# Causal mask of an attention kernel: from a TensorE product to an addition by VectorE in the bank

## The chip, the core and the metric

The kernel runs on one core of a Trainium2 chip. TensorE multiplies into the banks of PSUM, VectorE, ScalarE and GpSimd do the rest in SBUF and, the first two, in the banks; SyncE issues most DMAs. The metric is the device time of the core in microseconds (us).

## What is computed

The kernel is one block of a model: attention, a feed-forward layer, a state-space mixer and the feed-forward layer again, each on the layer-normed x and added to it. x is 8 x 512 x 1024 in float32. The change touches the attention alone, 32 heads of 32 columns with one head of keys and values:

```python
q = (x @ wq_w.T + wq_b).reshape(b, t, H, HD)        # H = 32, HD = 32, t = 512
k = (x @ wk_w.T + wk_b).reshape(b, t, HKV, HD)      # HKV = 1
v = (x @ wv_w.T + wv_b).reshape(b, t, HKV, HD)
scores = jnp.einsum('bqhd,bkd->bhqk', q, k1) / jnp.sqrt(jnp.float32(HD))
scores = jnp.where(jnp.tril(jnp.ones((t, t), dtype=bool)), scores, -jnp.inf)
weights = jax.nn.softmax(scores, axis=-1)
attn = jnp.einsum('bhqk,bkd->bqhd', weights, v1).reshape(b, t, H * HD)
return attn @ wo_w.T + wo_b
```

## The kernel before

The attention works through 64 groups G: 8 batches, and in each 8 groups of 4 heads (128 columns of q). A loop over steps M (`STEPS`, from -3 to 65) is written out once for each engine, so the order of each engine's instructions is fixed by hand. In step M, three groups are in flight: the query projection of group M + 2 (`q_part`), the scores of group M + 1 (`scores`, queries on the partitions, to find each row's maximum and part of its sum), the transposed scores of group M (`turned_scores`, keys on the partitions, shifted by the maximum) with their exponentials, and the weighted sums of group M - 1 (`weigh_first` to `weigh_fourth`).

The scores of a group come in 11 units (`S_UNITS`): four of 512 keys, four of 384, two of two heads with 256 keys, and one of four heads with 128. A unit lies in one of two banks (`S0` and the next), by turns. k is stored negated, so that the largest score is a minimum. For a unit TensorE runs one product a head (line 831) and then a product of an identity with `causal_r` (line 834), which adds a large positive number to the later keys of the diagonal block of every head in the bank. It raises `s_ready`. VectorE takes the row minimum into `top` (`tops`, line 659) and raises `s_used`. For the first 8 units ScalarE then runs exp over the bank with `top` as bias (`row_sum`, line 572): only its row sum (`den`) is wanted, and the exponentials themselves go to the tile `spent`, which nobody reads. TensorE may write a bank again when the unit two before it is done with (`den_done` for the first 8, `s_used` for the others).

At the end of a group `tops_turned` (line 850) transposes `top` on TensorE, after all 11 minima; `copy_rows` on ScalarE copies the result, and a DMA (`shift`) puts it into row 96 of `q_stack`, from where `turned_scores` (line 861) subtract it. ScalarE's `exps` (line 558) writes the weights `pt`, GpSimd clears their diagonal blocks (`cut`), and TensorE multiplies them with the values (line 868). VectorE's `invert`, `take_inverse` and `divide` (line 682) turn these sums into attention outputs, in which `att_done` is raised; `weigh_first` of the next step waits for it.

VectorE's order in a step M is: minima 0 and 1 of group M + 1, then (in four of the eight steps of a batch) the moments of a tile of the next batch's x, minima 2 and 3, that tile's normalisation, minima 4 and 5, the low half of q (`q_low`, line 688), minima 6 and 7, a reciprocal (line 668), minimum 8, a second reciprocal, a copy (line 671), minima 9 and 10, `den_invert`, and `divide`. Steps with M % 8 of 0 and 1 also run the output products of the batch before (`output`), behind everything else of the step; that with M % 8 = 6 runs the products for keys and values of the next batch (`kv_part`) and transposes of its x (line 795), some of which come before line 868; that with M % 8 = 5 takes in transposed x as well (line 647).

A feed-forward and mixer stage follows (from about 1700 us on); none of its code is touched.

## Time and profile before

| what | value |
|---|---|
| time, median of 3 runs | 2995.66 us (2991.35 to 2996.05) |
| profiled execution, span | 2999.3 us |
| TensorE busy | 2801.1 us, 93% |
| VectorE busy | 1620.4 us, 54% |
| ScalarE busy | 1159.1 us, 39% |
| GpSimd busy | 945.7 us, 32% |

The time is that of a run; the profile is one more execution, whose span from the first to the last instruction is given beside it. Busy shares are means over the whole span. The rows of TensorE have modelled ends: a product's record is longer than the time until the next one starts, so its cost is read from start to start.

### The profile page before, as it was taken

How to read it: one execution, taken by the hardware profiler on the slowest of the kernel's cores; microseconds unless marked ns; L12 is line 12 of the kernel's file. 1: busy time of each engine (PE TensorE's matmuls, PEld its weight loads, DVE VectorE, ACT ScalarE, POOL GpSimd, SP SyncE). 2: the span in 40 equal slices, each digit the busy share in tenths (PEclk: the TensorE clock that was granted, in tenths of full speed). 3: DMA queues.
4: the chain of work that ended last, by engine and by line, in shares of the span. 5: the costliest groups of instructions: out<-in, count | busy, mean ns of one | idle time of the engine just before them, and what ended most of it. 6: DMA issues, size and time to landing. Idle time of an engine off the chain costs nothing. (4 is left out here: it accounts for less than half of the span.)

```text
span 2999.3 us, 41858 instructions
## 1 busy us (share of the span) xinstructions
PE 2801.1 (93%) x15808; PEld 2116.6 (71%) x15808; DVE 1620.4 (54%) x2960; ACT 1159.1 (39%) x2509; POOL 945.7 (32%) x1460
## 2 busy tenths in 40 slices
PE   5888999999999999999999987999999999999988
PEld 3666767767777677676776565787878787878766
DVE  3453464553744645536444346666666666666653
ACT  3664365462744645627445012222222222222220
POOL 2333122121221222212213044444454444444422
PEclk8889999999999999999999888999999999999989
DMA  5765545544545454445354510010101010201011
GB/s 155 197 162 151 169 106 150 126 117 127 137 93 166 107 160 124 104 148 127 82 151 147 174 46 1 2 56 2 56 5 52 5 53 2 56 2 56 1 28 29
DMA packets 103626, 272.29 MB, mean 91 GB/s; under 512 B 12122, under 2 KB 23514, under 8 KB 101122
## 3 DMA queue, kind: packets, MB, share of 16 engines
q1 hardware_dynamic: 102706, 269.55, 33.2%
q8 instruction: 126, 2.06, 0.3%
q14 instruction: 74, 0.61, 0.1%
q10 hardware_dynamic: 720, 0.07, 0.0%
HBM read 168.40 MB, written 50.33 MB: 73 GB/s over the span
## 5 line engine op out<-in xcount | busy, mean ns | idle before, releaser
L659 DVE TENSOR_REDUCE top<-ps_attn 128x1 fp32r<-128x512 f32 (+3 forms) x704 | 441.0, 639 | 466.4 <-PE ps_attn L834 460.5
L471 POOL TENSOR_SCALAR_AFFINE_SELECT pt<-pt 128x512 f32<-128x512 f32 x256 | 163.3, 649 | 954.6 <-ACT pt L558 954.6
L558 ACT ACTIVATE pt<-ps_attn 128x512 f32<-128x512 f32 (+1 forms) x704 | 381.3, 559 | 137.3 <-PE ps_attn L861 137.0
L1555 PE MATMUL ps_mixer<-m_w_hi,m_xt_hi 128*128 128x512 f32 x1024 | 423.5, 414 | 1.6 <-DVE m_xt_lo L1337 1.6
L572 ACT ACTIVATE spent<-ps_attn,top 128x512 f32<-128x512 f32 (+1 forms) x512 | 325.4, 636 | 240.1 <-DVE top L659 238.3
L1557 PE MATMUL ps_mixer<-m_w_lo,m_xt_hi 128*128 128x512 f32 x1024 | 407.9, 398 | 0.0
L1556 PE MATMUL ps_mixer<-m_w_hi,m_xt_lo 128*128 128x512 f32 x1024 | 407.9, 398 | 0.0
L861 PE MATMUL ps_attn<-q_stack,k_stack 97*128 97x512 f32 (+3 forms) x1024 | 298.8, 352 | 38.5 <-DMA q_stack<-top_rows 28.5
L831 PE MATMUL ps_attn<-k_stack,q_stack 96*128 96x512 f32 (+3 forms) x1024 | 304.9, 350 | 28.4 <-DMA q_stack<-q_lo 14.5
L1237 ACT CAST m_xt_hi<-ps_mixer 128x512 fp32r<-128x512 f32 x192 | 104.2, 589 | 494.1 <-PE ps_mixer L1550 494.0
L831 PEld LDWEIGHTS ps_attn<-k_stack,q_stack 96*128 96x128 f32 x1024 | 176.1, 195 | 105.2 <-ACT spent L572 49.9
L861 PEld LDWEIGHTS ps_attn<-q_stack,k_stack 97*128 97x128 f32 x1024 | 175.1, 192 | 100.2 <-DMA q_stack<-top_rows 36.2
L1555 PEld LDWEIGHTS ps_mixer<-m_w_hi,m_xt_hi 128*128 128x128 f32 x1024 | 199.3, 195 | 63.5 <-issue 15.6
L761 PE MATMUL ps_attn<-xn_hi,wq_hi 128*128 128x512 f32 x512 | 226.0, 441 | 6.4 <-DVE xn_lo L647 6.4
L1556 PEld LDWEIGHTS ps_mixer<-m_w_hi,m_xt_lo 128*128 128x128 f32 x1024 | 198.5, 194 | 42.5 <-issue 3.4
L1557 PEld LDWEIGHTS ps_mixer<-m_w_lo,m_xt_hi 128*128 128x128 f32 x1024 | 197.4, 193 | 43.2
L1337 DVE TENSOR_TENSOR m_xt_lo<-ps_mixer,m_xt_hi 128x512 fp32r<-128x512 f32 x192 | 124.4, 686 | 176.4 <-ACT m_xt_hi L1237 176.1
L708 DVE TENSOR_TENSOR xr<-ps_attn,xr 128x512 f32<-128x512 f32 x64 | 44.3, 692 | 304.3 <-PE ps_attn L763 304.3
L762 PE MATMUL ps_attn<-xn_hi,wq_lo 128*128 128x512 f32 x512 | 206.6, 404 | 0.0
L763 PE MATMUL ps_attn<-xn_lo,wq_hi 128*128 128x512 f32 x512 | 206.0, 402 | 0.0
L1184 POOL TENSOR_TENSOR m_xs<-m_xs,m_p_base_b 128x256 f32<-128x256 f32 x256 | 182.6, 745 | 65.8 <-DVE m_xn L1330 59.1
L868 PE MATMUL ps_attn<-pt,v_sb 128*32 128x512 f32 (+3 forms) x2048 | 194.7, 452 | 1.4 <-DVE att L682 0.9
(216 smaller groups left out, 5114.3 us busy)
## 6 DMA issues: line engine op xcount, KB each, us to landing
xr<-in_a_x SPq DMA_DIRECT2D x64, 512.0 KB, 6.7
q_stack<-q_hi SPq DMA_DIRECT2D x128, 256.0 KB, 5.6
wq_hi<-wq_split SPq DMA_DIRECT2D x56, 512.0 KB, 3.9
wq_lo<-wq_split SPq DMA_DIRECT2D x56, 512.0 KB, 4.6
q_stack<-q_lo SPq DMA_DIRECT2D x64, 256.0 KB, 6.8
wo_hi<-wo_split SPq DMA_DIRECT2D x8, 2048.0 KB, 8.4
wo_lo<-wo_split SPq DMA_DIRECT2D x8, 2048.0 KB, 12.8
x<-xr SPq DMA_DIRECT2D x32, 512.0 KB, 2.8
```

Of the source, the lines that this page charges most:

```text
L558: nc.scalar.activation(pt[k][:, heads[0]:heads[0] + len(heads), :].rearrange("p j t -> p (j t)"), ps[:, ST0 + n % 2, 0:width * len(heads)] ...
L572: nc.scalar.activation(spent[:, 0:width], ps[:, S0 + n % 2, 0:width], ACT.Exp, scale=-1.0, bias=top[:, j * TILES + i:j * TILES + i + 1].bi ...
L659: nc.vector.tensor_reduce(out, ps[:, S0 + n % 2, 0:width * len(heads)].rearrange("p (j k) -> p j k", k=width), AX.X, ALU.min).then_inc(s_u ...
L761: nc.tensor.matmul(out, a_hi, b_hi, start=first, stop=False)
L762: nc.tensor.matmul(out, a_lo, b_hi, start=False, stop=False)
L763: return nc.tensor.matmul(out, a_hi, b_lo, start=False, stop=last)
L831: nc.tensor.matmul(bank[:, m * width:(m + 1) * width], q_stack[0:KROWS, G % 3, j, i * P:(i + 1) * P], k_stack[0:KROWS, b % 2, 0:width], st ...
L861: mm = nc.tensor.matmul(ps[:, ST0 + n % 2, m * width:(m + 1) * width], k_stack[:, b % 2, k * P:(k + 1) * P], q_stack[:, G % 3, j, k * P:T] ...
L868: mm = nc.tensor.matmul(ps[j * HEAD:(j + 1) * HEAD, bank, k * P:end], side, pt[k][:, j, 0:end - k * P], start=(k == 0), stop=(k == TILES - ...
L1555: nc.tensor.matmul(out, a_hi, b_hi, start=first, stop=False)
L1556: nc.tensor.matmul(out, a_lo, b_hi, start=False, stop=False)
L1557: return nc.tensor.matmul(out, a_hi, b_lo, start=False, stop=last)
```

## The change

`causal_r` becomes a plain float32 tile `later_keys` with the same content. TensorE's product with the identity is gone; the last product of a unit raises `s_ready`. VectorE first adds `later_keys` in place to the diagonal block of every head in the bank, raises `s_masked`, waits for it, and takes the minimum as a second instruction. `row_sum` writes its exponentials back into the bank they came from, and the tile `spent` is gone; the constants that were loaded into it stand in `att` until they are used. `kvs_turned` is merged into `bkv_ready`.

```diff
--- before.py
+++ after.py
@@ -176,15 +176,15 @@
         stats, mean_var = sb("stats", [P, TILES, 2, 6]), sb("mean_var", [P, TILES, 2])
         var_eps, inv_std, neg_half = sb("var_eps", [P, TILES]), sb("inv_std", [P, TILES]), sb("neg_half", [P, 1])
         bo_rows = sb("bo_rows", [P, D])
-        bq_sb, bkv_sb, kvs_sb, bkv_scaled = sb("bq_sb", [P, CH]), sb("bkv_sb", [P, 1]), sb("kvs_sb", [P, 1]), sb("bkv_scaled", [P, 1])
-        ident_r, causal_r = sb("ident_r", [P, P], F32R), sb("causal_r", [P, P], F32R)
-        spent, den, den_inv = sb("spent", [P, T]), sb("den", [P, 2, GH]), sb("den_inv", [P, 2, 2, GH])
-        identb_sb, causal_sb = spent[:, 0:P // 2].bitcast(BF16), spent[:, P // 2:P].bitcast(BF16)
+        bq_sb, kvs_sb, bkv_scaled = sb("bq_sb", [P, CH]), sb("kvs_sb", [P, 1]), sb("bkv_scaled", [P, 1])
+        ident_r, later_keys = sb("ident_r", [P, P], F32R), sb("later_keys", [P, P])
+        den, den_inv = sb("den", [P, 2, GH]), sb("den_inv", [P, 2, 2, GH])
+        identb_sb, causal_sb, bkv_sb = att[:, 0, 0:P // 2].bitcast(BF16), att[:, 0, P // 2:P].bitcast(BF16), att[:, 0, P:P + 1]
         ps = ctx.enter_context(nc.psum_tensor("ps_attn", [P, 8, HALF], F32))
         ident_f = ident_r[:, :].bitcast(F32)
 
         params_in, wkv_in, wkv_hi_done, wkv_lo_done = sem("params_in"), sem("wkv_in"), sem("wkv_hi_done"), sem("wkv_lo_done")
-        setup_done, kvs_turned, bkv_ready, mask_done = sem("setup_done"), sem("kvs_turned"), sem("bkv_ready"), sem("mask_done")
+        setup_done, bkv_ready, mask_done = sem("setup_done"), sem("bkv_ready"), sem("mask_done")
         wq_raw_in, wqhi_done, wqlo_done, wq_out = sem("wq_raw_in"), sem("wqhi_done"), sem("wqlo_done"), sems("wq_out", 2)
         xr_in = sems("xr_in", TILES)
         stats_done, mv_done, eps_done, std_done, xn_done = (sem("stats_done"), sem("mv_done"), sem("eps_done"), sem("std_done"),
@@ -249,8 +249,8 @@
                 inv_sqrt(pool, 0, 0)
                 inv_sqrt(pool, 0, 1)
                 pool.wait_ge(params_in, 5 * DMA)
-                nc.gpsimd.tensor_scalar(kvs_sb[0:KROWS, :], kvs_sb[0:KROWS, :], -1.0, None, ALU.mult).then_inc(kvs_turned, 1)
-                pool.wait_ge(kvs_turned, 1)
+                nc.gpsimd.tensor_scalar(kvs_sb[0:KROWS, :], kvs_sb[0:KROWS, :], -1.0, None, ALU.mult).then_inc(bkv_ready, 1)
+                pool.wait_ge(bkv_ready, 1)
                 nc.gpsimd.tensor_tensor(bkv_scaled[:, :], bkv_sb[:, :], kvs_sb[:, :], ALU.mult).then_inc(bkv_ready, 1)
                 inv_sqrt(pool, 0, 2)
                 inv_sqrt(pool, 0, 3)
@@ -265,7 +265,7 @@
                 act.wait_ge(wkv_in, DMA)
                 nc.scalar.copy(wkv_hi[:, :, :], wkv_raw).then_inc(wkv_hi_done, 1)
                 wq_high(act, 0)
-                act.wait_ge(bkv_ready, 1)
+                act.wait_ge(bkv_ready, 2)
                 act.wait_ge(params_in, 5 * DMA)
 
             @block.vector
@@ -276,7 +276,7 @@
                 dve.wait_ge(params_in, 5 * DMA)
                 nc.vector.memset(k_stack[KROWS:KROWS + 1, :, :].bitcast(F32), -1.0).then_inc(mask_done, 1)
                 nc.vector.tensor_copy(ident_r[:, :], identb_sb).then_inc(mask_done, 1)
-                nc.vector.tensor_scalar(causal_r[:, :], causal_sb, -1.0, None, ALU.mult).then_inc(mask_done, 1)
+                nc.vector.tensor_scalar(later_keys[:, :], causal_sb, -1.0, None, ALU.mult).then_inc(mask_done, 1)
                 normalise(dve, 0, 1)
                 dve.wait_ge(wkv_hi_done, 1)
                 nc.vector.tensor_tensor(wkv_lo[:, :, :], wkv_raw, wkv_hi[:, :, :].bitcast(F32), ALU.subtract).then_inc(wkv_lo_done, 1)
@@ -285,6 +285,7 @@
                 normalise(dve, 0, 2)
                 normalise(dve, 0, 3)
                 dve.wait_ge(setup_done, 3)
+                dve.wait_ge(mask_done, 3)
 
             @block.tensor
             def _(pe):
@@ -298,6 +299,7 @@
         wq_in, q_ready, qhi_done, qlo_done, qs_in = sems("wq_in", 2), sem("q_ready"), sem("qhi_done"), sem("qlo_done"), sem("qs_in")
         s_ready, s_used, top_done, topt_ready, top_rows_done, top_in = (sem("s_ready"), sem("s_used"), sem("top_done"),
                                                                         sem("topt_ready"), sem("top_rows_done"), sem("top_in"))
+        s_masked = sem("s_masked")
         st_ready, exp_done, sel_done, a_done, b_done = (sem("st_ready"), sem("exp_done"), sem("sel_done"), sem("a_done"),
                                                         sem("b_done"))
         den_done, den_inv_done, den_rep_done = sem("den_done"), sem("den_inv_done"), sem("den_rep_done")
@@ -569,7 +571,8 @@
                         act.wait_ge(den_inv_done, G)
                     if u or G:
                         act.wait_ge(den_done, SUMMED * G + u)
-                    nc.scalar.activation(spent[:, 0:width], ps[:, S0 + n % 2, 0:width], ACT.Exp, scale=-1.0,
+                    bank = ps[:, S0 + n % 2, 0:width]
+                    nc.scalar.activation(bank, bank, ACT.Exp, scale=-1.0,
                                          bias=top[:, j * TILES + i:j * TILES + i + 1].bitcast(F32),
                                          accum_out=den[:, i - (TILES - SUM_TILES), j:j + 1]).then_inc(den_done, 1)
 
@@ -656,8 +659,12 @@
                         if u == 0 and G:
                             dve.wait_ge(topt_ready, G)
                         out = top[:, 0:GH * TILES].rearrange("p (j i) -> p j i", i=TILES)[:, heads[0]:heads[0] + len(heads), i]
-                        nc.vector.tensor_reduce(out, ps[:, S0 + n % 2, 0:width * len(heads)].rearrange("p (j k) -> p j k", k=width),
-                                                AX.X, ALU.min).then_inc(s_used, 1)
+                        bank = ps[:, S0 + n % 2, 0:width * len(heads)].rearrange("p (j k) -> p j k", k=width)
+                        diagonal = bank[:, :, i * P:width]
+                        nc.vector.tensor_tensor(diagonal, diagonal, later_keys[:, None, :].to_broadcast([P, len(heads), P]),
+                                                ALU.add).then_inc(s_masked, 1)
+                        dve.wait_ge(s_masked, n + 1)
+                        nc.vector.tensor_reduce(out, bank, AX.X, ALU.min).then_inc(s_used, 1)
 
                 def invert(G, part):
                     if part == 0:
@@ -828,11 +835,9 @@
                             pe.wait_ge(s_used, n - 1)
                     bank = ps[:, S0 + n % 2, 0:width * len(heads)]
                     for m, j in enumerate(heads):
-                        nc.tensor.matmul(bank[:, m * width:(m + 1) * width], q_stack[0:KROWS, G % 3, j, i * P:(i + 1) * P],
-                                         k_stack[0:KROWS, b % 2, 0:width], start=(m == 0), stop=False)
-                    diagonal = bank.rearrange("p (j k) -> p j k", k=width)[:, :, i * P:width]
-                    nc.tensor.matmul(diagonal, ident_r[:, :], causal_r[:, None, :].to_broadcast([P, len(heads), P]),
-                                     start=False, stop=True).then_inc(s_ready, 1)
+                        mm = nc.tensor.matmul(bank[:, m * width:(m + 1) * width], q_stack[0:KROWS, G % 3, j, i * P:(i + 1) * P],
+                                              k_stack[0:KROWS, b % 2, 0:width], start=(m == 0), stop=(m == len(heads) - 1))
+                    mm.then_inc(s_ready, 1)
 
                 def tops_turned(G):
                     pe.wait_ge(s_used, U * (G + 1))
```

## Rows read from the trace of the kernel before

**Rows 1.** The page, busy time, share of the span and instructions of each engine.

```profile
PE 2801.1 (93%) x15808; PEld 2116.6 (71%) x15808; DVE 1620.4 (54%) x2960; ACT 1159.1 (39%) x2509; POOL 945.7 (32%) x1460
```

**Rows 2.** By stretch: span, PE, PEld, DVE, ACT, POOL busy, granted clock, DMA share, GB/s.

```profile
979.33:996.48 17.15, 17.02 (x119) 12.24 (x118) 12.09 (x22) 12.12 (x31) 4.86 (x9) 1.00 0.60 139
996.48:1015.59 19.11, 17.83 (x132) 13.40 (x131) 14.10 (x26) 14.17 (x35) 5.57 (x10) 1.00 0.46 98
1015.59:1045.96 30.37, 26.90 (x165) 18.98 (x166) 14.69 (x25) 15.30 (x36) 4.20 (x6) 1.00 0.40 96
1045.96:1063.06 17.10, 16.98 (x118) 12.27 (x119) 10.14 (x17) 11.78 (x29) 3.83 (x7) 1.00 0.71 170
1063.06:1102.40 39.34, 38.94 (x216) 30.16 (x214) 13.11 (x22) 13.16 (x32) 16.02 (x14) 1.00 0.26 61
1213.18:1246.60 33.42, 29.93 (x165) 20.71 (x166) 14.68 (x25) 15.29 (x36) 4.19 (x6) 0.90 0.36 88
```

**Rows 3.** VectorE in order of time: start, us, line, operation, idle before and releaser.

```profile
989.56 0.74 DVE L688 SCALAR_TENSOR_TENSOR q_lo<-ps_attn,bq_sb,q_hi 128x512 fp32r<-128x512 f32 x1
990.87 1.02 DVE L659 TENSOR_REDUCE top<-ps_attn 128x1 fp32r<-128x384 f32 x2 [0.57 <-PE ps_attn L834]
991.81 0.95 DVE L668 RECIPROCAL att<-ps_attn 128x128 f32<-128x128 f32 x1
992.86 0.69 DVE L659 TENSOR_REDUCE top<-ps_attn 128x2 fp32r<-128x512 f32 x1
993.47 0.95 DVE L668 RECIPROCAL att<-ps_attn 128x128 f32<-128x128 f32 x1
994.33 0.36 DVE L671 COPY att<-ps_attn 128x256 f32<-128x256 f32 x1
994.61 1.36 DVE L659 TENSOR_REDUCE top<-ps_attn 128x2 fp32r<-128x512 f32 x2
...
995.99 0.64 DVE L682 TENSOR_TENSOR att<-ps_attn,att 128x512 f32<-128x512 f32 x1
998.80 0.69 DVE L659 TENSOR_REDUCE top<-ps_attn 128x1 fp32r<-128x512 f32 x1 [2.17 <-PE ps_attn L834]
```

**Rows 4.** TensorE in order of time, the first `weigh_first` products of two steps.

```profile
979.61 1.06 PE L868 MATMUL ps_attn<-pt,v_sb 128*32 128x512 f32 x8
...
996.77 1.06 PE L868 MATMUL ps_attn<-pt,v_sb 128*32 128x512 f32 x8
```

**Rows 5.** TensorE in order of time, a mask product among its neighbours.

```profile
982.18 0.40 PE L831 MATMUL ps_attn<-k_stack,q_stack 96*128 96x512 f32 x1
982.42 0.22 PE L834 MATMUL ps_attn<-causal_r,ident_r 128*128 128x128 f32 x1
982.48 0.45 PE L761 MATMUL ps_attn<-xn_hi,wq_hi 128*128 128x512 f32 x1
982.76 0.39 PE L762 MATMUL ps_attn<-xn_hi,wq_lo 128*128 128x512 f32 x1
983.00 0.40 PE L763 MATMUL ps_attn<-xn_lo,wq_hi 128*128 128x512 f32 x1
```

**Rows 6.** VectorE's groups by shape behind 1800 us: busy, mean ns, idle before.

```profile
L1337 DVE TENSOR_TENSOR m_xt_lo<-ps_mixer,m_xt_hi 128x512 fp32r<-128x512 f32 x180 | 116.6, 686 | 164.2 <-ACT m_xt_hi L1237 164.0
...
L1429 DVE TENSOR_TENSOR m_decay<-m_decay,m_dt_mask 128x256 f32<-128x256 f32 x16 | 6.6, 415 | 0.0
...
L1437 DVE TENSOR_TENSOR m_weight<-m_weight,m_d_diag 128x128 f32<-128x128 f32 x16 | 4.7, 292 | 0.6
```

**Rows 7.** VectorE in order of time, an instruction that waits for the two before it.

```profile
983.29 1.27 DVE L223 BATCH_NORM_STATS2 stats<-xr 128x6 f32<-128x512 f32 x2
984.60 0.21 DVE L225 BATCH_NORM_AGGREGATE mean_var<-stats 128x2 f32<-128x12 f32 x1
```

**Rows 8.** TensorE in order of time, ahead of a key and value step.

```profile
1213.18 0.30 PE L850 MATMUL ps_attn<-ident_r,top 128*128 128x128 f32 x1 [1.26 <-issue]
...
1214.63 1.08 PE L795 MATMUL ps_attn<-ident_r,xr 128*128 128x128 f32 x4 [0.69 <-ACT top_rows L544]
```

## The prediction, made before the change was run

> **What bounds the kernel now.** I read first the busy shares of the page, then a table of single steps of the attention loop, then the order of time of TensorE and of VectorE in one step. On the page TensorE is busy 93% of the span and VectorE 54% [rows 1]. That invites the conclusion that work moved from the one to the other is gained. The average hides the step. The loop over M has four kinds of steps after its start [rows 2]: a plain one (17.10 us, VectorE busy 10.14), one with the moments of a coming batch (17.15 us, 12.09), the two with the output products (39.34 us, 13.11), and the one with the key and value products (30.37 us). The fourth row, 19.11 us with 14.10 busy, is a step with moments that also takes in transposed x.
>
> In the step from 979.33 to 996.48 the end is what matters. From the query's low half at 989.56 on, VectorE works almost without a gap: minima of units 6 and 7, a reciprocal of 0.95 us, unit 8, a second reciprocal, a copy, units 9 and 10, and `divide`, which ends at 995.99 + 0.64 = 996.63 [rows 3]. TensorE's next `weigh_first` (line 868) waits for `att_done`, which is that division. It begins at 996.77, 0.14 us behind it [rows 4]. So a step closes as a loop: `weigh_first` at 979.61, TensorE through the scores up to unit 6, VectorE's tail from 990.87 to 996.63, `weigh_first` at 996.77. That is 17.16 us, of which 11.26 are paced by TensorE and 5.76 by VectorE's tail. The change takes from the first stretch and gives to the second.
>
> **What the change takes away.** Line 834 issues 11 products a step, and TensorE's rows show what one of 128 columns costs [rows 5]: from its start 982.42 to the next 982.48 is 0.06, and the product behind it takes 982.76 - 982.48 = 0.28 until the next starts, where 0.235 is usual (982.18 to 982.42, 982.76 to 983.00). That is 0.06 + 0.045 = 0.105 us, much less than the busy time of the record. Eight of these are 0.84. For the two of 256 columns I estimate 0.12 each, and for the one of 512 columns a full product's 0.235 + 0.045 = 0.28. Together this is 1.36 us a step, and 87 us in 64 steps if TensorE were the only limit.
>
> **What it adds.** VectorE gets 11 additions a step, each followed by a minimum that waits for it through `s_masked`. No instruction of the kernel before adds in place in a bank, but additions of the same sizes stand in the mixer [rows 6]: 0.292 us for 128x128, 0.415 for 128x256, and 0.686 for 128x512 with one input from a bank. A write to a bank is not in the trace. I take it at the price of a write to SBUF, and bound it by 0.1 less and 0.1 more an instruction, about the 0.08 that two instructions in line overlap (below). The wait: the `bn_aggr` that waits for two `bn_stats` starts at 984.60, and the pair ends at 983.29 + 1.27 = 984.56, thus some 0.035 us behind [rows 7]. In line without a wait the next instruction starts some 0.08 before the last one ends: the copy at 994.33 begins ahead of 993.47 + 0.95 = 994.42, and the next minimum at 994.61 ahead of 994.33 + 0.36 = 994.69 [rows 3]. So an addition and its wait put 0.292 + 0.035 = 0.33 us in front of a single head's minimum, 0.45 for two heads, 0.72 for four. That is 8 x 0.33 + 2 x 0.45 + 0.72 = 4.26 us a step. Everything of VectorE is queued behind that wait: the minimum, the query's low half, both reciprocals, the division, and with it TensorE's `weigh_first`.
>
> A rule speaks on this wait. The Trainium skill ("VectorE: DVE Perf Modes", section "The DRAIN you can't avoid") holds that chaining without semaphores saves nothing, that a semaphore costs nothing extra. This trace differs by 0.035 + 0.08 = 0.115 us a dependent start. By the rule the tail below would be 5 x 0.115 = 0.6 us shorter a step, and the sum 42 x 0.6 = 25 us lower. I go by the rows.
>
> **A plain step, new.** The minimum of unit 6 began 11.26 us after `weigh_first`. Six masks before it are gone (-0.63), and the addition can begin when the last score product ends rather than the mask (-0.07). Some of this comes back, since a bank is now held longer: minimum, exponential with row sum, and only then the next scores into it. It comes free 0.33 - 0.07 = 0.26 later, and TensorE arrives for it two masks or 0.21 earlier, 0.47 in all where there is no slack now. The bounds are 0 and the whole 0.63; I take 0.2, less than half of the 0.47. Addition 6 thus starts at 10.76. From there the tail is 5.76 plus additions 6 to 10, 2 x 0.33 + 2 x 0.45 + 0.72 = 2.28, less 0.2 for the gaps that stand in it now (991.81 + 0.95 against 992.86, [rows 3]): 7.84. With the 0.14 to `weigh_first` a step takes 18.74 us against 17.1, 1.6 more.
>
> **A step with moments, new.** Here VectorE's own work is the floor: 12.09 + 4.26 = 16.35 [rows 2], and the turn from the division over `weigh_first` and the first scores to the first addition, which today is 2.17 idle [rows 3] and becomes 2.10. That is 18.45. Some idle time can't be filled, since TensorE paces units 4 to 6 and ScalarE the query's low half; I put it at 0.45. So 18.9 against 17.15, 1.75 more.
>
> **The other steps.** In each of the two output steps TensorE has 22 us of output products behind the tail [rows 2], which hide it. What TensorE saves is gained there, less its waits for the banks: I take 0.4 of 1.36. The key and value step has the same cover (VectorE busy 14.69 of 30.37) and its start is a chain of short waits: 0.3 gained. Ahead of it TensorE already idles 1.26 and 0.69 us [rows 8], and the tail of the step before it makes that about 2 us more. Where today's gap there met a lower clock, the step took 33.42 instead of 30.37 at a mean granted clock of 0.90, so a fifth of it at 1.2 GHz [rows 2]. I charge half of the 3.05 in each such step: 1.5.
>
> **Unhidden or nought.** The exponentials of line 572 write to the bank instead of `spent`. They are as many and as wide. They matter only for when a bank is free, which is in the 0.2 above; `den_invert` needs them long before it runs. Three set-up edits (another home for the constants, `bkv_ready` counted to 2, a wait for `mask_done`) happen once, under loads. The Trainium skill ("ScalarE: Activation LUTs", section "Step-by-step: what each stage is for") calls PSUM the faster destination for ScalarE. No row here shows such a write; by it the 0.2 would go, 42 x 0.2 = 8 us off the sum.
>
> **Sum.** There are 64 groups, so 63 turns from one step to the next: 14 output steps, 7 key and value steps, 28 with moments, 14 plain ones (among them the last five and the first two). 28 x 1.75 + 14 x 1.6 = 71; -14 x 0.4 = -6; -7 x 0.3 + 7 x 1.5 = +8. Together +73 us. The mixer behind it is untouched. The profiled execution spans 2999.3 us, 0.1% over the median of the three runs, 2995.66; I add the sum to the median: 3069 us, +2.4%.
>
> **Rivals.** (a) The gaps cost clock as well. In each of 42 steps TensorE now idles some 1.6 us ahead of lines 850 and 868. The gaps of 1.26 and 0.69 us had half clock behind them in one step of [rows 2, 8]; the like step of 30.37 us kept 1.00. If every second of the 42 lost 1.5 us and could hide a third of it, that is 21 x 1.0 = 21 us, and in all of them 42; with additions 0.1 dearer in a bank (5 in the tail, 42 x 0.5 = 21) it is 3090 to 3135. Against it: VectorE, not TensorE, would set those steps, which hides part. (b) The minimum starts 0.08 before its addition ends, as in line, instead of 0.035 behind it (42 x 5 x 0.115 = 24 us), or additions in a bank are 0.1 cheaper (21 us): 3045 to 3050, and both 3025. By [rows 7] the wait does cost. The section of the Trainium skill on the DRAIN, named above, would have the first half of this rival. (c) Not slower: TensorE stays the bound, because VectorE takes the additions into its idle time. The place is the division ahead of `weigh_first`: if the tail grows by less than about 0.75 us, the time that TensorE's stretch loses (0.63 + 0.07 less 0.2) and the gaps of 0.2 cover it; that needs an addition with its wait at a third of 0.33 us. Where it grows by nothing and the division holds nobody up, the whole 87 us go: 2909. VectorE's 46% of idle time speaks for it; that this idle time lies in the first two thirds of a step and in the output steps speaks against it. (d) Gain and loss cancel, 2996: an addition with its wait at a third of my price.
>
> **How the numbers follow.** Forecast as summed, 3050 to 3090: 0.58. (a) 0.22, (b) 0.12, (c) 0.06, (d) 0.02. The range leaves out (c), (d) and the edges of (a) and (b): 3033 to 3130. About 0.2% is what a measurement of this kernel can tell from no change: faster 0.06, the same 0.03, slower 0.91.
>
> **What would show it.** Right: plain steps of 18.6 to 18.9 us, line 868 still 0.14 behind the division, TensorE idle 1.3 to 1.8 us ahead of line 850 for VectorE's minimum, additions of 0.29 us with the minimum 0.035 behind. Wrong: steps near 16, idle time of VectorE ahead of unit 8, additions under 0.15 us, or a granted clock well under 1.00 in the plain steps.

## The result, and the profile after

The changed kernel takes 3110.52 us, the median of 4 runs (3105.94 to 3115.46), against 2995.86 before (2991.35 to 2996.21, 4 runs): 1.0387 times, 95% interval 1.0364 to 1.0411. The prediction said 3069 us, with a range from 3033 to 3130. The direction and the range held. The time itself lies outside the 3050 to 3090 of the likeliest case and inside those of rival (a), the one about the clock.

The busy shares of the page answer [rows 1]. Each row below is of the changed kernel unless a sentence says otherwise.

```profile
PE 2860.2 (92%) x15104; PEld 2065.0 (66%) x15104; DVE 1856.8 (60%) x3664; ACT 1153.6 (37%) x2509; POOL 949.4 (31%) x1460
```

TensorE lost 704 products and is busy 59 us longer. Where the time went is seen first by two stretches, the attention loop (from the first `tops_turned` to the last) and what follows it. The columns are those of [rows 2]: span, busy time of PE, PEld, DVE, ACT and POOL, granted clock, DMA share, GB/s. First the kernel before:

```profile
65.62:1625.94 1560.32, 1477.09 (x9123) 1089.37 (x9121) 777.50 (x1311) 820.19 (x1962) 375.93 (x470) 0.98 0.51 137
1625.94:2999.26 1373.32, 1289.84 (x6549) 1000.18 (x6549) 816.86 (x1606) 317.60 (x516) 553.94 (x970) 0.94 0.12 36
```

Then the changed kernel:

```profile
67.25:1749.46 1682.21, 1544.92 (x8428) 1044.71 (x8428) 1010.70 (x2006) 815.11 (x1962) 379.96 (x472) 0.91 0.47 127
1749.46:3111.90 1362.44, 1280.86 (x6549) 994.23 (x6549) 816.12 (x1606) 316.95 (x514) 553.46 (x968) 0.95 0.12 37
```

The loop is 121.9 us longer. What follows it, the mixer above all, has the same 6549 products and is 10.9 us shorter at a slightly higher clock; no line of the change lies there. In the loop the clock fell from 0.98 to 0.91. With two levels, 2.4 and 1.2 GHz, that is about 2 x 0.09 x 1682 = 303 us at half clock, against 2 x 0.02 x 1560 = 62; the two digits of the clock leave some 17 us open in each.

Single steps answer [rows 2]. In order: a step with moments, the same kind again, one that also takes in transposed x, the key and value step, a plain step, an output step, and a later one with moments:

```profile
1014.13:1033.22 19.09, 16.91 (x108) 10.78 (x108) 15.72 (x34) 12.09 (x30) 5.57 (x9) 1.00 0.52 125
1033.22:1053.58 20.36, 18.38 (x107) 10.95 (x107) 15.70 (x34) 12.09 (x30) 4.94 (x8) 0.92 0.51 118
1053.58:1076.46 22.88, 18.97 (x120) 12.11 (x121) 18.20 (x38) 14.09 (x34) 4.95 (x8) 0.93 0.38 82
1076.46:1109.62 33.16, 28.66 (x155) 19.26 (x155) 18.55 (x36) 15.40 (x36) 3.93 (x5) 0.90 0.35 88
1109.62:1127.96 18.34, 17.69 (x107) 11.47 (x107) 13.26 (x28) 11.74 (x29) 4.77 (x8) 0.93 0.66 159
1127.96:1170.83 42.87, 41.82 (x204) 30.68 (x204) 17.29 (x34) 12.89 (x31) 15.18 (x12) 0.91 0.24 56
...
1230.81:1251.31 20.50, 19.63 (x107) 12.00 (x107) 15.70 (x34) 12.09 (x30) 6.01 (x9) 0.83 0.49 117
```

The first row is the step as forecast: 19.09 us where 18.9 was said, at a clock of 1.00. The last is the same kind of step with the same VectorE work (15.70 busy) at 0.83, and takes 1.4 us more. Before, all steps of [rows 2] but one had 1.00. Of all 28 steps with moments 24 stood at 1.00 before, and 4 do now.

VectorE in order of time answers [rows 3]; start, us, line, operation, idle before and releaser:

```profile
1016.85 0.30 DVE L664 TENSOR_TENSOR ps_attn<-ps_attn,later_keys 128x128 f32<-128x128 f32 x1 [2.11 <-PE ps_attn L838]
1017.18 0.69 DVE L667 TENSOR_REDUCE top<-ps_attn 128x1 fp32r<-128x512 f32 x1
...
1024.31 0.30 DVE L664 TENSOR_TENSOR ps_attn<-ps_attn,later_keys 128x128 f32<-128x128 f32 x1 [0.69 <-PE ps_attn L838]
...
1026.03 0.30 DVE L664 TENSOR_TENSOR ps_attn<-ps_attn,later_keys 128x128 f32<-128x128 f32 x1 [0.17 <-PE ps_attn L838]
...
1031.74 0.69 DVE L664 TENSOR_TENSOR ps_attn<-ps_attn,later_keys 128x512 f32<-128x512 f32 x1
1032.47 0.69 DVE L667 TENSOR_REDUCE top<-ps_attn 128x4 fp32r<-128x512 f32 x1
...
1033.18 0.64 DVE L689 TENSOR_TENSOR att<-ps_attn,att 128x512 f32<-128x512 f32 x1
1037.22 0.30 DVE L664 TENSOR_TENSOR ps_attn<-ps_attn,later_keys 128x128 f32<-128x128 f32 x1 [3.40 <-PE ps_attn L838]
```

Between the first addition and the division VectorE idles for only two gaps, 0.69 and 0.17 us, beside 0.04 ahead of each minimum. Its own work is the floor of this step. The turn from a division to the next first addition is 2.11 ahead of this step and 3.40 behind it. TensorE at those two turns shows why, and answers [rows 4]:

```profile
1014.13 0.33 PE L855 MATMUL ps_attn<-ident_r,top 128*128 128x128 f32 x1 [1.22 <-DVE top L667]
1014.89 1.06 PE L873 MATMUL ps_attn<-pt,v_sb 128*32 128x512 f32 x8 [0.42 <-DVE att L689]
...
1033.22 0.47 PE L855 MATMUL ps_attn<-ident_r,top 128*128 128x128 f32 x1 [1.21 <-DVE top L667]
1033.97 1.94 PE L873 MATMUL ps_attn<-pt,v_sb 128*32 128x512 f32 x8 [0.28 <-DVE att L689]
```

Both times TensorE waits for VectorE, ahead of `tops_turned` (now line 855) for the last minimum and ahead of `weigh_first` (now 873) for the division, 1.64 and 1.49 us in all. Behind the second wait the same eight products take 1.94 us where they took 1.06. Two stretches of that step name the level:

```profile
1033.22:1036.60 3.38, 3.10 (x17) 0.87 (x17) 0.61 (x2) 0.77 (x2) 1.61 (x2) 0.50 0.07 12
1036.60:1040.00 3.40, 3.34 (x17) 2.37 (x14) 2.71 (x6) 1.56 (x5) 0.00 (x0) 1.00 0.94 336
```

VectorE's groups by shape answer [rows 6]: busy, mean ns, idle before.

```profile
L664 DVE TENSOR_TENSOR ps_attn<-ps_attn,later_keys 128x128 f32<-128x128 f32 x512 | 151.0, 295 | 316.1 <-PE ps_attn L838 311.5
L664 DVE TENSOR_TENSOR ps_attn<-ps_attn,later_keys 128x256 f32<-128x256 f32 x128 | 53.0, 414 | 16.9 <-PE ps_attn L838 16.8
L664 DVE TENSOR_TENSOR ps_attn<-ps_attn,later_keys 128x512 f32<-128x512 f32 x64 | 44.2, 691 | 9.2 <-PE ps_attn L838 9.0
```

0.295, 0.414 and 0.691 us, where 0.292, 0.415 and 0.686 were charged.

### The profile page after: what moved, and what is told of

Same layout as the page of the kernel before. It is cut to its first block and busy times, and to the rows that moved or that the text cites. A ratio compares the mean times of both kernels' runs of the same rounds, so it can differ in the third digit from the quotient of the medians.

```text
span 3111.9 us, 41155 instructions
## 1 busy us (share of the span) xinstructions
PE 2860.2 (92%) x15104; PEld 2065.0 (66%) x15104; DVE 1856.8 (60%) x3664; ACT 1153.6 (37%) x2509; POOL 949.4 (31%) x1460
## 5 line engine op out<-in xcount | busy, mean ns | idle before, releaser
L667 DVE TENSOR_REDUCE top<-ps_attn 128x1 fp32r<-128x512 f32 (+3 forms) x704 | 452.8, 643 | 24.1
L664 DVE TENSOR_TENSOR ps_attn<-ps_attn,later_keys 128x128 f32<-128x128 f32 (+2 forms) x704 | 248.2, 353 | 342.2 <-PE ps_attn L838 337.3
L575 ACT ACTIVATE ps_attn<-ps_attn,top 128x512 f32<-128x512 f32 (+1 forms) x512 | 311.7, 609 | 337.3 <-DVE top L667 333.4
L838 PE MATMUL ps_attn<-k_stack,q_stack 96*128 96x512 f32 (+3 forms) x1024 | 322.8, 368 | 54.7 <-ACT ps_attn L575 34.9
L866 PE MATMUL ps_attn<-q_stack,k_stack 97*128 97x512 f32 (+3 forms) x1024 | 323.1, 375 | 27.9 <-DMA q_stack<-top_rows 16.3
L866 PEld LDWEIGHTS ps_attn<-q_stack,k_stack 97*128 97x128 f32 x1024 | 183.5, 207 | 98.4 <-ACT pt L560 34.0
L1560 PEld LDWEIGHTS ps_mixer<-m_w_hi,m_xt_hi 128*128 128x128 f32 x1024 | 197.0, 192 | 62.5 <-issue 15.6
L873 PE MATMUL ps_attn<-pt,v_sb 128*32 128x512 f32 (+3 forms) x2048 | 223.7, 512 | 10.5 <-DVE att L689 9.5
L768 PE MATMUL ps_attn<-xn_hi,wq_hi 128*128 128x512 f32 x512 | 218.1, 426 | 6.6 <-DVE xn_lo L650 6.6
```

The source lines that it names most:

```text
L575: nc.scalar.activation(bank, bank, ACT.Exp, scale=-1.0, bias=top[:, j * TILES + i:j * TILES + i + 1].bitcast(F32), accum_out=den[:, i - (T ...
L664: nc.vector.tensor_tensor(diagonal, diagonal, later_keys[:, None, :].to_broadcast([P, len(heads), P]), ALU.add).then_inc(s_masked, 1)
L667: nc.vector.tensor_reduce(out, bank, AX.X, ALU.min).then_inc(s_used, 1)
L768: nc.tensor.matmul(out, a_hi, b_hi, start=first, stop=False)
L838: mm = nc.tensor.matmul(bank[:, m * width:(m + 1) * width], q_stack[0:KROWS, G % 3, j, i * P:(i + 1) * P], k_stack[0:KROWS, b % 2, 0:width ...
L866: mm = nc.tensor.matmul(ps[:, ST0 + n % 2, m * width:(m + 1) * width], k_stack[:, b % 2, k * P:(k + 1) * P], q_stack[:, G % 3, j, k * P:T] ...
```

## The experiments

Two questions stood. Is the excess over the forecast the clock, or is VectorE's tail longer than it was summed? And which of the forecast's prices hold?

### Dummy products in TensorE's wait

Theory: the excess is clock. If TensorE works while it waits ahead of line 855, the clock stays, and the steps fall to what VectorE sets. The wait is moved behind the dummy products, whose results nobody reads.

```diff
+        FILLERS = {0: 6, 3: 6, 4: 6, 5: 6, 6: 14}
-                    pe.wait_ge(s_used, U * (G + 1))
                     b, g = divmod(G, GROUPS)
 ...
+                    for _ in range(FILLERS.get(g, 0) if G else 0):
+                        nc.tensor.matmul(ps[:, MISC, P:HALF], wkv_hi[:, 0, :], wkv_hi[:, 1:4, :], start=True, stop=True)
+                    pe.wait_ge(s_used, U * (G + 1))
                     nc.tensor.transpose(ps[:, MISC, 0:P], top[:, :].bitcast(F32), ident_f).then_inc(topt_ready, 1)
```

> The changed kernel, with products that nobody reads put into TensorE's wait ahead of line 855: 6 of 384 columns (about 0.18 us each, 1.1 us in all) in steps with M % 8 of 0, 3, 4 and 5, and 14 in those with 6. Theory: half of the 115 us is the lower clock that TensorE gets because it idles 1.2 + 0.4 us at the end of a step. The steps of 20.6 us at a granted clock of 0.83 then go to about 19.1 at 1.00, and the whole to 3040 to 3075 us. Rival: VectorE sets these steps, the clock costs nothing there, and what is above 18.5 us a step comes from elsewhere; then 3105 to 3125 us.

Measured: 3088.50 us (3077.91 to 3094.82), 1.0322 times the kernel before (1.0282 to 1.0362). Between the two ranges. The 14 products ahead of each key and value step were the miss:

```profile
1059.84 4.85 PE L856 MATMUL ps_attn<-wkv_hi 128*128 128x384 f32 x14 [2.60 <-DVE xn_lo L651]
```

In TensorE's order they stand behind another wait for VectorE, 2.60 us for the low half of x, so they don't fill a wait but follow it, and their 4.85 us lie on the path. The step that ends with them takes 25.63 us. The second version leaves out `6: 14`, and the same step is 21.02. (The key and value step behind the 14 products gained by them: 30.66 us at 0.93, against 32.20 at 0.91 in the second version.)

> As the run named fill, but without the 14 products in steps with M % 8 of 6: there they stood behind the wait for the transposed x and lengthened the step (25.63 us for the step that ends there against 23.04). Theory: the other fillers keep the granted clock at 1.00 in the steps of 18.3 to 19.1 us, so this takes the rest of the clock's share: 3065 to 3085 us. Rival: those steps gain as in fill, but the steps with M % 8 of 5 and 6 fall back into the lower clock and give all of it back: 3090 to 3110.

Measured: 3072.20 us (3062.80 to 3081.29), 1.0256 (1.0230 to 1.0282), as the theory had it, so 38 us less than the changed kernel with more work on TensorE. Its loop, and then steps that stand above too (the late step with moments, the key and value step, the plain one, the output step):

```profile
67.16:1689.93 1622.77, 1494.38 (x8614) 1038.01 (x8615) 1008.37 (x2004) 816.53 (x1962) 379.94 (x471) 0.96 0.49 131
...
1196.02:1215.10 19.08, 18.05 (x113) 11.81 (x114) 15.71 (x34) 12.09 (x30) 5.57 (x9) 1.00 0.53 126
1048.06:1080.26 32.20, 28.34 (x154) 18.73 (x155) 18.59 (x36) 15.52 (x36) 3.88 (x5) 0.91 0.38 90
1080.26:1098.61 18.35, 17.66 (x113) 11.82 (x113) 13.26 (x28) 11.74 (x29) 4.82 (x8) 1.00 0.65 159
1098.61:1138.36 39.75, 38.56 (x204) 28.81 (x204) 17.26 (x34) 12.89 (x31) 15.17 (x12) 1.00 0.26 61
```

The late step with moments is 19.08 at 1.00, where it was 20.50 at 0.83, with the same VectorE work. The output step is 39.75 instead of 42.87. The loop is 62.5 us over the one before, at 0.96. The plain step doesn't move (18.34 and 18.35). In the changed kernel its slow stretch lies at its end, under VectorE's tail, and runs on into the output step, which paid. The late step with moments begins in the same way:

```profile
1125.50:1127.96 2.46, 2.34 (x7) 1.52 (x7) 2.39 (x7) 1.11 (x2) 1.27 (x2) 0.50 0.16 18
1127.96:1132.00 4.04, 3.75 (x18) 1.36 (x19) 0.61 (x2) 0.78 (x2) 2.69 (x3) 0.50 0.14 34
...
1227.80:1230.81 3.01, 2.89 (x12) 2.07 (x10) 2.94 (x8) 2.04 (x4) 1.44 (x3) 0.50 0.34 39
1230.81:1234.58 3.77, 3.49 (x18) 1.15 (x19) 0.61 (x2) 0.78 (x2) 2.67 (x3) 0.50 0.16 34
```

Those four rows are of the changed kernel. At these two turns the clock had fallen 2.5 to 3 us ahead of `tops_turned`, and the slower products left only 0.12 us of the wait for the last minimum that is 1.2 at the turns shown above. With the dummy products both stretches are gone. So some 38 of the 41.5 us above the forecast are the clock's, shown by giving them back.

### The division ahead of units 9 and 10

Theory: with the division earlier, `weigh_first` stops waiting for it. Units 9 and 10 then come behind it on VectorE.

```diff
                         take_inverse(M - 1)
+                        divide(M - 1)
 ...
-                    if inside(M - 1):
-                        divide(M - 1)
```

> The changed kernel, with the division of a group moved ahead of units 9 and 10 on VectorE, so that line 873 no longer waits for it behind the last minimum. Theory: the step closes as a loop over VectorE's tail; line 855 still waits for the last minimum, now 0.2 us behind it, and line 873 follows at once, 0.4 us a step earlier in 42 steps: 17 us, and some of the lower clock with it, 3070 to 3095 us. Rival: the division holds nobody up, 3105 to 3120 us.

Measured: 3126.82 us (3124.76 to 3129.12), 1.0454 (1.0414 to 1.0495), slower than the change itself and above both ranges. My theory fell. TensorE at a turn in this kernel, here behind a plain step (ahead of two steps with moments the wait is 2.01 as well):

```profile
1135.87 0.33 PE L854 MATMUL ps_attn<-ident_r,top 128*128 128x128 f32 x1 [2.01 <-DVE top L667]
1136.13 1.06 PE L872 MATMUL ps_attn<-pt,v_sb 128*32 128x512 f32 x8
```

The 0.42 ahead of `weigh_first` is gone, but `tops_turned` stands in front of it in TensorE's order and waits for the last minimum, which the division now delays: 2.01 where it was 1.22, and 1.22 + 0.42 with the wait behind it. The loop of the changed kernel closes over two points that lie one behind the other, the last minimum and then the division. In the kernel before, [rows 4] showed only the second.

### No mask at all

The addition and its wait are left out, and TensorE makes no mask either, so that later keys stay in the maximum and the row sum.

```diff
-                        nc.vector.tensor_tensor(diagonal, diagonal, later_keys[:, None, :].to_broadcast([P, len(heads), P]),
-                                                ALU.add).then_inc(s_masked, 1)
-                        dve.wait_ge(s_masked, n + 1)
```

> The changed kernel without any mask: neither TensorE nor VectorE adds it, so later keys stay in the row maximum and the row sum. Theory: the time falls under that of before by what TensorE's 11 mask products cost, 1.36 us a step from start to start, 87 us in all: 2900 to 2925 us. If a mask product costs its whole busy record (183 us in all), 2810 to 2850. Rival: what is slow is not the addition but the exponentials in the bank; then it stays above 2995.

Measured: 2941.45 us (2937.80 to 2947.32), 0.9836 (0.9802 to 0.9869). Between the ranges again: the mask products cost some 50 us, not 87.

```profile
951.28:967.56 16.28, 16.10 (x109) 10.70 (x107) 12.02 (x22) 12.09 (x31) 4.96 (x9) 1.00 0.63 146
...
1071.73:1110.22 38.49, 38.04 (x203) 28.70 (x204) 12.86 (x21) 11.81 (x29) 2.89 (x5) 1.00 0.59 198
```

16.28 is 0.87 less than the 17.15 of [rows 2]. The output step is the second of its batch; it takes 38.49, and before those took 39.27 to 40.41. In the step with moments VectorE's tail is unchanged but for its gaps and closes the step, so the masks behind unit 6 give nothing back. What is left is the six masks before the tail, the 0.07 and the tail's 0.2 of gaps, which the prediction had as 0.63 + 0.07 + 0.2 = 0.90.

### An addition that nobody waits for

The same additions write to an SBUF tile that is never read, and the minimum doesn't wait for them (later keys stay in the maximum and the row sum). What is taken away is the dependent start, and the write to the bank.

```diff
-                        nc.vector.tensor_tensor(diagonal, diagonal, later_keys[:, None, :].to_broadcast([P, len(heads), P]),
+                        if n:
+                            dve.wait_ge(s_masked, n)
+                        nc.vector.tensor_tensor(spare[:, 0:len(heads), :], diagonal, later_keys[:, None, :].to_broadcast([P, len(heads), P]),
                                                 ALU.add).then_inc(s_masked, 1)
-                        dve.wait_ge(s_masked, n + 1)
```

> The changed kernel, but the addition writes its sum to an SBUF tile that nobody reads, so the minimum needs no wait for it; later keys stay in the maximum and the row sum. The additions cost VectorE what they did. Theory: the wait costs 0.035 + 0.08 us an addition, with five in the tail 0.6 us a step, 42 steps: 25 us, and some lower clock with it: 3065 to 3090 us. Rival: the wait costs nothing extra, since the next instruction can't begin before the one ahead is through in any case: 3105 to 3120.

Measured: 3049.24 us (3036.25 to 3051.85), 1.0183 (1.0166 to 1.0200): 61 us less than the change, more than either range allowed for. Three rows of VectorE's tail in a plain step:

```profile
1085.97 0.68 DVE L669 TENSOR_REDUCE top<-ps_attn 128x2 fp32r<-128x512 f32 x1
1086.57 0.68 DVE L667 TENSOR_TENSOR spare<-ps_attn,later_keys 128x512 f32<-128x512 f32 x1
1087.17 0.68 DVE L669 TENSOR_REDUCE top<-ps_attn 128x4 fp32r<-128x512 f32 x1
```

The minimum begins 0.08 before its addition ends (1086.57 + 0.68 = 1087.25); in the changed kernel it begins 0.04 behind (1031.74 + 0.69 = 1032.43, then 1032.47). The difference is 0.12 a dependent start, where 0.115 was charged. The write itself hardly matters:

```profile
L667 DVE TENSOR_TENSOR spare<-ps_attn,later_keys 128x128 f32<-128x128 f32 x512 | 147.1, 287 | 340.1 <-PE ps_attn L840 337.0
```

287 ns to SBUF and 295 in place in the bank. Two steps that stand above as well, the one with moments (19.09 there) and the plain one (18.34):

```profile
979.36:997.68 18.32, 16.62 (x108) 10.75 (x108) 14.71 (x34) 12.27 (x30) 6.16 (x9) 1.00 0.57 130
1070.11:1087.90 17.79, 16.52 (x107) 10.64 (x107) 12.20 (x28) 11.87 (x29) 4.77 (x8) 1.00 0.68 164
```

The plain step is 0.55 shorter, which is the tail's five starts (5 x 0.12 = 0.6). The one with moments is 0.77 shorter: where VectorE's work is the floor, starts ahead of the tail count too, and my expectation had left those out. Shorter waits of TensorE also gave part of the clock back (0.944 over the execution, where the changed kernel has 0.924); how much of the 61 us that is, this run doesn't separate. By the two steps shown, the starts alone would give an estimated 28 x 0.77 + 14 x 0.55 = 29 us, about half.

### The exponentials, back in the tile and alone in the bank

In the changed kernel, the exponentials go to a tile again; in the kernel before, they go to the bank and nothing else changes:

```diff
-                    nc.scalar.activation(bank, bank, ACT.Exp, scale=-1.0,
+                    nc.scalar.activation(spent[:, 0:width], bank, ACT.Exp, scale=-1.0,
```

> The changed kernel, but the exponentials with row sum go to an SBUF tile again, as in the kernel before. Theory: where they go decides only when a bank is free, so 3105 to 3125 us, if anything later than the changed kernel by up to 8 us. Rival: exponentials that are written into the bank collide with other traffic there and make up a good part of the 115 us; then 3000 to 3080.

```diff
-                    nc.scalar.activation(spent[:, 0:width], ps[:, S0 + n % 2, 0:width], ACT.Exp, scale=-1.0,
+                    nc.scalar.activation(ps[:, S0 + n % 2, 0:width], ps[:, S0 + n % 2, 0:width], ACT.Exp, scale=-1.0,
```

> The kernel before with one edit: the exponentials that are only summed go back into their own bank instead of into the SBUF tile; masks stay TensorE products. Theory (the in-bank exponentials change nothing that is on the path; the run that put the tile back into the changed kernel could not tell it from nought): 2988 to 2998 us, within 0.2% of the kernel before. Each such exponential is shorter by about 0.03 us, so a bank comes free 0.03 to 0.06 us earlier, and the waits of TensorE's weight load on ScalarE's exponentials (49.9 us in total, 143 of them, before) fall by at most some 5 us. Rival (the bank is written twice in the time that another unit uses the port, and this costs): 3002 to 3015 us, with those waits at 55 us or more.

Measured: 3119.32 us (3107.71 to 3122.87), 1.0422 (1.0383 to 1.0461), whose interval overlaps that of the change; and 2995.32 us (2990.25 to 3001.28, 12 runs), 1.0009 (0.9996 to 1.0022). Alone, this part of the change is worth nothing that can be measured; in the changed kernel the 8.8 us between the two medians can't be told from nothing. The group in the changed kernel, and then in the kernel before:

```profile
L575 ACT ACTIVATE ps_attn<-ps_attn,top 128x512 f32<-128x512 f32 x256 | 169.4, 662 | 283.5 <-DVE top L667 282.6
```

```profile
L572 ACT ACTIVATE spent<-ps_attn,top 128x512 f32<-128x512 f32 x256 | 176.1, 688 | 212.1 <-DVE top L659 210.7
```

An exponential into its bank is 26 ns shorter. The waits of TensorE for those banks did not fall (49.9 us before, 50.8 with the exponentials alone in the bank), so this half of my expectation missed.

### Fewer masks on VectorE

If VectorE masks only units that it takes long before its tail, TensorE should gain and the tail shouldn't grow. These are the kernel before with VectorE's addition for some units, first 0, 1, 4 and 5, then 0 to 5 (the set-up edits of the change come with it):

```diff
+                        if u in ON_DVE:
+                            diagonal = bank[:, :, i * P:width]
+                            nc.vector.tensor_tensor(diagonal, diagonal, causal_r[:, :].bitcast(F32)[:, None, :].to_broadcast([P, len(heads), P]),
+                                                    ALU.add).then_inc(s_masked, 1)
+                            dve.wait_ge(s_masked, len(ON_DVE) * G + ON_DVE.index(u) + 1)
 ...
+                    if u in ON_DVE:
+                        mm.then_inc(s_ready, 1)
+                        return
```

> The kernel before, with VectorE masking units 0, 1, 4 and 5 only, and TensorE the others; exponentials go to SBUF as before. Theory: a mask product counts only where it stands ahead of unit 6 (nomask: 0.83 us a step, 50 in all), and VectorE has idle time ahead of these four units in every kind of step, so 4 x 0.105 us a step are gained and the tail stays 5.76: 2960 to 2980 us. Rival: any addition delays the bank and the tail behind it: 2996 or more.

> As split0145, with units 2 and 3 masked by VectorE too. Theory: in plain and output steps two more products are gained, 0.2 us each step; in the 28 steps with moments VectorE's idle time (2.75 us ahead of units 1 to 6) just takes 6 x 0.33 = 2.0, or is late for unit 6 by up to 0.5: 2955 to 2990 us, close to split0145. Rival: with moments the idle time does not suffice and each such step loses over 0.7 us: above 2990.

Measured: 2994.80 us, 0.9995 (0.9978 to 1.0011), and 2990.46 us, 0.9982 (0.9970 to 0.9995). Both theories missed: the first time lies between its ranges, the second at the lower edge of the rival's. The four masks should have given 4 x 0.105 = 0.42 us a step, and a step with moments, the first kind of [rows 2], shrank from 17.15 to 17.03 only. The waits of TensorE's weight load for a bank that ScalarE still reads show where the rest went: us in total, times, longest. The kernel before, the changed kernel, and the one with units 0, 1, 4 and 5:

```profile
PEld ps_attn L831 <- ACT spent L572: 49.9, 143, 2.2
```

```profile
PEld ps_attn L838 <- ACT ps_attn L575: 115.7, 231, 2.9
```

```profile
PEld ps_attn L839 <- ACT spent L575: 72.0, 177, 2.5
```

The masks gave TensorE 64 x 0.42 = 27 us and the banks took 22 back. TensorE's weight loads in such a step show the place:

```profile
976.74 0.19 PEld L839 LDWEIGHTS ps_attn<-k_stack,q_stack 96*128 96x128 f32 x1 [0.50 <-ACT spent L575]
```

This is unit 2, which needs unit 0's bank. Unit 0 opens the step, right behind the turn; its addition and dependent minimum hold the bank longer, and TensorE is back for it after unit 1. So the last version masks units 1, 4 and 5 on VectorE, with the exponentials in the bank:

> The kernel before with VectorE masking units 1, 4 and 5 of each step alone, TensorE all others, and the exponentials in their bank. Theory (with unit 0 masked by VectorE as well, TensorE gave back most of its 0.42 us a step in a wait for unit 0's bank, 72.0 us of such waits in total against 49.9; without it, unit 2 finds its bank free): the three masks' 0.31 us a step are kept in the greater part, 0.15 to 0.3 us in 63 steps, 2976 to 2988 us, and the waits for banks stay under 62 us. Rival (whatever mask goes to VectorE, the bank comes free later by the time of an addition and a dependent start, and the loop of VectorE's tail is as long as before): 2990 to 3000 us, with waits for banks of 65 us or more.

Measured: 2978.43 us (2972.36 to 2986.81, 8 runs), 0.9942 (0.9923 to 0.9961), faster than both kernels.

```profile
PEld ps_attn L839 <- ACT ps_attn L575: 58.1, 181, 2.5
```

```profile
968.05:984.89 16.84, 16.70 (x116) 11.65 (x115) 13.00 (x25) 12.03 (x31) 4.89 (x9) 1.00 0.61 142
...
1033.95:1050.72 16.77, 16.65 (x115) 11.76 (x116) 10.95 (x20) 11.53 (x29) 3.83 (x7) 1.00 0.71 173
```

16.84 and 16.77 against 17.15 and 17.10 of [rows 2]: 0.31 and 0.33, the whole of 3 x 0.105. Since the exponentials alone are worth nothing, the gain is put down to the units chosen; the same units with the exponentials in the tile were not run.

## Why the prediction was right, and what it mis-sized

**The bound and the loop: right.** VectorE's tail closes the step, and idle time elsewhere in VectorE's 46% didn't help. The one view that misled here is the average of [rows 1], as the prediction said.

**The price of an addition: right**, to 0.005 us in all three shapes; the bounds of 0.1 on either side weren't needed.

**The dependent start: right.** 0.04 behind instead of 0.08 ahead. The Trainium skill ("VectorE: DVE Perf Modes", section "The DRAIN you can't avoid") says of eight copies in a row that a semaphore costs nothing extra. The same section of the Trainium skill lets a next instruction that isn't held start earlier. By the first of these, taken as a rule, the run with unread additions would equal the change but for the write, 8 to 24 ns each; the steps shown there are 0.55 and 0.77 us shorter. The measurement decides.

**The sum, kind by kind.** These are the steps from one `tops_turned` to the next, in us against the kernel before, in the profiled executions (0.1 less in all than the stretch above, whose ends lie a little wider):

| steps | forecast | the change | dummy products, second version |
|---|---|---|---|
| 28 with moments | +49 | +60.8 | +38.5 |
| 14 plain | +22 | +22.7 | +20.1 |
| 14 output | -6 | +25.6 | -2.4 |
| 7 key and value | +8 | +12.7 | +6.3 |
| all 63 | +73 | +121.8 | +62.5 |

**A step with moments and a plain step: right.** 19.08 to 19.09 against 18.9. A plain step takes 18.35 at full clock with no wait ahead of its `weigh_first`; with the 0.43 that the next one waits, the loop from `weigh_first` to `weigh_first` is 18.8 against 18.74. TensorE's idle time ahead of `tops_turned` is 1.2 where 1.3 to 1.8 was said, and the rest of it, some 0.4, lies ahead of `weigh_first`.

**Output steps: too optimistic.** I took 0.4 off each. At full clock the one above is 39.75 against 39.34, and these 0.4 are the wait of 0.43 that the loop of the plain step has just been charged with; without it the first output step of a batch is level. The seven second ones are 2 us shorter together. TensorE's waits for banks are the place of the gain that I had counted there: 1.5 us in the step above with dummy products, 0.6 in the same step before.

**Key and value steps: somewhat low.** +1.2 was charged on average, and 1.8 was measured in the change, at a clock of 0.90 (0.9 with the dummy products). The wait ahead of `tops_turned` there grew from 1.26 to 2.65, by 1.4 where about 2 was said.

**Nought for the exponentials: right**, by the run that moves them alone. The Trainium skill's page "ScalarE: Activation LUTs" ("Step-by-step: what each stage is for") agrees on the sign, 26 ns; the 8 us by it are not shown.

**The clock: the term that was mis-sized.** The sum charged 7 x 1.5 = 10 us, in the key and value steps alone. Filling the waits gave back 38 us (3110.5 to 3072.2), and 59 between the two profiled loops (the profiled execution with the dummy products lies 9 us below the median of its kernel). Of these 59, 28 lay in the output steps, 22 in the steps with moments, 6 in the key and value steps and 3 in the plain ones. The prediction said that the products of the output steps hide the tail. They do, but the slow stretch that begins under the tail of the step ahead runs into the start of the output step, and nothing hides that: 42.87 instead of 39.75. These steps alone make 31 of the 49 us by which the loop exceeds the sum.

I had the mechanism as rival (a) and marked it down with the sentence that VectorE, not TensorE, would set those steps, which hides part. The rows say why it hides only what lies ahead of the turn. Behind the turn the slow stretch falls on `weigh_first` and the first scores, the part of the loop that TensorE paces: at 1033.22 the first addition then waits 3.40 instead of 2.11 [rows 3 answered above], and the step is 1.27 longer, so there the whole loss is on the path. That the time is what rival (a) gives for all its 42 steps, 73 + 42 = 115 us, is luck: it counted no output step. That the loop with the dummy products came out at +62.5, where the sum without its 10 is 63, is partly luck too. Four steps with moments at the start stood at 0.86 to 0.87 before and are 9 us shorter there; the other 24 are 2.0 us longer, not 1.75. The prediction saw a lost stretch in [rows 2], 33.42 instead of 30.37, and should have asked of each new wait of over 1 us what work stands behind it. Its own sign of being wrong, a clock well under 1.00 in the plain steps, came in part: 0.93.

**The ceiling of rival (c): wrong by its own steps.** 87 us counted masks that the tail hides (and its 0.12 for 256 columns left out the 0.045 that the other two prices have); without any mask the kernel is 50 us faster. The prediction's own 0.90 a step gives 63 x 0.90 = 57.

**Open.** Two turns with nearly the same waits, 1.22 + 0.42 and 1.21 + 0.28, stood at 1.00 and at 0.50 behind them, and at others the clock fell ahead of the turn. Which waits lose the clock wasn't found, only that filling those ahead of `tops_turned` gives it back.

## What to carry to other kernels

Ask of each wait that a change puts on an engine whose clock can fall which instructions stand right behind it: if they are on the path, the loss is paid in full, and work in the wait got it back here. Cover at the end of a step is no cover for a slow start of the next. Work moved to an engine with idle time is free only in the places where nothing is queued behind it, and a bank, too, must come free no later: three units of eleven moved gained 0.6%, all eleven lost 3.9%. Of two waits that close a loop one behind the other, shortening the second by delaying the first makes it longer.

## What the runs showed of the hardware

An addition by VectorE in place in a bank takes 1 to 6% longer than one that writes to SBUF (295 and 287 ns for 128x128, 414 and 390 for 128x256, 691 and 682 for 128x512). An instruction of VectorE that waits for the one before it starts 0.12 us later than one that doesn't (0.04 behind its end, against 0.08 ahead of it). An exponential of 128x512 written back to its own bank takes 662 ns, and 688 into SBUF. Around waits of TensorE of 1.21 and 0.28 us its granted clock stood at 0.50 for 3.4 us, and that step was 1.27 us longer than one at 1.00 throughout; around waits of 1.22 and 0.42 us it stayed at 1.00.
